# One-level products split by halves of a block's nodes, turns as 64 by 32 products, and two work banks, in a two-layer graph kernel

## What is computed

```python
def _L0_gnn_ref(x, L_scaled, weight, bias):       # K = 4
    Tx_prev2, Tx_prev1 = x, L_scaled @ x
    out = Tx_prev2 @ weight[0] + Tx_prev1 @ weight[1]
    for k in range(2, K):
        Tx_curr = 2.0 * (L_scaled @ Tx_prev1) - Tx_prev2
        out = out + Tx_curr @ weight[k]
        Tx_prev2, Tx_prev1 = Tx_prev1, Tx_curr
    return out + bias
def _L1_gnn_ref(x, adj, kernel, bias):
    support = adj @ poincare_expmap(x, 1.0)
    return poincare_logmap(support, 1.0) @ kernel + bias
h = jnp.maximum(_layernorm(x, axis=-1), 0.0)
x = x + _L0_gnn_ref(h, adj, L0_gnn_weight, L0_gnn_bias)
h = jnp.maximum(_layernorm(x, axis=-1), 0.0)
x = x + _L1_gnn_ref(h, adj, L1_gnn_kernel, L1_gnn_bias)
```

## Time and profile before

| | |
|---|---|
| median of 3 runs | 1762.29 us (1762.16 to 1763.82) |
| profiled execution | 1763.04 us, of which the span is 1760.9 us |
| PE busy | 1712.7 us (97% of the span) |
| DVE busy | 1276.1 us (72%) |
| ACT, POOL busy | 251.1 us (14%), 166.8 us (9%) |
| loads of blocks | 626 of 1 MB, queue's share of the DMA engines 93.9% |
| mean granted TensorE clock | 0.996 |

### The profile page before, as it was taken

The page is one execution under the profiler, slowest core; times in us unless marked ns, Lnnn a source line. Parts: engine busy times, 40 slices in busy tenths (PEclk is TensorE's granted clock), DMA queues, the critical chain, the costliest instruction groups (busy, mean ns, idle before and its releaser), DMA issues.

```text
span 1760.9 us, 57416 instructions
## 1 busy us (share of the span) xinstructions
PE 1712.7 (97%) x26188; PEld 940.1 (53%) x26188; DVE 1276.1 (72%) x1948; ACT 251.1 (14%) x468; POOL 166.8 (9%) x229
## 2 busy tenths in 40 slices
PE   7979999999999999999999999999999999999997
PEld 4423456666666665566666654345555444454444
DVE  7102686776888687688888886588878877786856
ACT  1000111111211011121110002222110110010024
POOL 0001000000000011211011000111001100010003
PEclk9999999999999999999999999999999999999999
DMA  9999999999999987889999986799999999999995
GB/s 371 421 421 421 420 419 419 411 409 419 402 402 394 400 298 274 335 321 330 339 332 336 338 329 267 288 362 395 419 419 419 418 416 416 418 407 419 419 420 230
DMA packets 94976, 664.54 MB, mean 377 GB/s; under 512 B 11408, under 2 KB 13712, under 8 KB 14608
## 3 DMA queue, kind: packets, MB, share of 16 engines
q1 hardware_dynamic: 93744, 660.64, 93.9%
q10 hardware_dynamic: 992, 0.23, 0.1%
HBM read 658.74 MB, written 2.10 MB: 375 GB/s over the span
## 4 chain that ended last, share of the span: by engine, by line
PE 81%; DVE 8%; DMA 8%; issue 2%; SPq 1%; POOL 0%; DVEq 0%; ACT 0%
PE own_bank L768 23%; PE row_bank L768 15%; PE work_bank L823 14%; PE row_bank L701 10%; PE work_bank L768 9%; DMA ring<-adj_blocks 8%; PE turned L900 2%; DVE ring L1081 2%; PE row_bank L808 1%; DVE ring L1085 1%; PE work_bank L784 1%; PE own_bank L844 1%; PE work_bank L844 1%; PE work_bank L712 1%; DVE partial L1116 1%
## 5 line engine op out<-in xcount | busy, mean ns | idle before, releaser
L1081 DVE TENSOR_TENSOR ring<-ring 128x1024 f32<-128x1024 f32 x318 | 392.9, 1236 | 106.7 <-PE own_bank L768 42.3
L768 PE MATMUL own_bank<-ring 128*32 128x256 f32 x4960 | 427.9, 379 | 0.3
L768 PE MATMUL own_bank<-ring,nodes 128*32 128x256 f32 x3720 | 380.8, 379 | 1.3 <-DVE ring L1081 1.3
L823 PE MATMUL work_bank<-ring,nodes 128*32 128x512 f32 (+1 forms) x2744 | 324.9, 593 | 6.8 <-DVE nodes L1274 5.1
L768 PE MATMUL row_bank<-ring 128*32 128x256 f32 x3488 | 300.4, 379 | 0.1
L768 PEld LDWEIGHTS own_bank<-ring 128*32 128x32 f32 x4960 | 246.3, 110 | 91.2 <-DVE ring L1085 2.2
L701 PE MATMUL row_bank<-ring,nodes 128*32 128x512 f32 (+1 forms) x1712 | 264.1, 597 | 19.1 <-DMA ring<-adj_blocks 16.1
L768 PE MATMUL row_bank<-ring,nodes 128*32 128x256 f32 x2616 | 266.3, 379 | 2.6 <-POOL ring L647 1.7
L768 PEld LDWEIGHTS own_bank<-ring,nodes 128*32 128x32 f32 x3720 | 201.9, 110 | 101.5 <-issue 43.9
L1085 DVE TENSOR_TENSOR ring<-ring 128x512 f32<-128x512 f32 x318 | 227.3, 715 | 10.9
L1087 DVE TENSOR_TENSOR ring<-ring 128x512 f32<-128x512 f32 x318 | 226.6, 713 | 10.9
(11 more groups left out here) (159 smaller groups left out, 1175.6 us busy)
## 6 DMA issues: line engine op xcount, KB each, us to landing
ring<-adj_blocks SPq DMA_DIRECT2D x626, 1024.0 KB, 11.3
out<-resid SPq DMA_DIRECT2D x16, 128.0 KB, 2.1
resid<-x SPq DMA_DIRECT2D x7, 256.0 KB, 12.0
resid<-x SPq DMA_DIRECT2D x2, 128.0 KB, 3.9
w_raw<-cheb_weight ACTq DMA_DIRECT2D x2, 64.0 KB, 8.4
bias<-cheb_bias ACTq DMA_DIRECT2D x1, 32.0 KB, 3.5
bias<-hyp_bias ACTq DMA_DIRECT2D x1, 32.0 KB, 3.9
w_raw<-hyp_kernel ACTq DMA_DIRECT2D x2, 16.0 KB, 9.3
```

The lines of the kernel that those rows point to most:

```text
L768: done = nc.tensor.matmul(bank[lane:lane + H, columns], left(a, h, level), right[b][:, h, :], start=first and k < 2, stop=k == 6, tile_pos ...
L823: done = nc.tensor.matmul(bank[lane:lane + size, :], nodes[:, c * C + k, A if level == 3 else B, part:part + size], data[:, k, :], start=k ...
L1081: nc.vector.tensor_tensor(first_two(n, block), block[:, :, N2].rearrange("p (k h) n -> p k h n", k=2), block[:, 0:2, :].rearrange("p h (k ...
```

## The change

1. One-level visits put nodes 0 to 255 of the row into partitions 0 to 63 and nodes 256 to 511 into 64 to 127, each with all four chunks summed: 16 products of 256 columns where there were 8 of 512, into half a bank. Sums of one level are so 128 by 256 in place of 128 by 512 or 64 by 512; where `partial` keeps a level by halves of the partitions (levels 1 to 3) an add becomes two of 64 by 256 (`to_levels`, `to_halves`).
2. ScalarE's copies at SUM and OWN are gone, with their semaphore; VectorE does the whole of `acc`, which is half as large.
3. A turn, and H_TERM, is 16 products of 64 by 32: both halves of the partitions at once, into the two banks of a pair, over two chunks each in place of four chunks one after the other.
4. There are two work banks; the third is the second bank of `turned`, which is used by AGAIN visits alone, and only with no turn within two visits. A bank with an OWN or column-13 visit is held until its JOIN. Level 4 turns have three pairs of banks where there were five banks.
5. Panels begin at rows 2, 4, 8 and 12. Level 1 has 38 JOINs where there were 24, with 323 fast visits in place of 318 and 7 plain BOTH visits in place of 12. The slots for sums are given up after row 0.
6. In the third sweep the OWN visits of rows 5 to 7 stand at the row's end as those of rows 8 and later do, EXPAND's features count as known one visit later, and the JOIN of level 3 adds in the kept sum.

The core of the diff:

```diff
-PANEL, FAST_BELOW, FAST_FROM, LATE_FROM = 4, 12, 5, 8
+FAST_BELOW, FAST_FROM, LATE_FROM = 12, 5, 8
+PANELS = (2, 4, 8, 12)
...
         def expand():
-            follow(1, ("EXPAND", row), known_now)
+            follow(1, ("EXPAND", row), lambda: follow(1, None, known_now))
...
-            visits_to_turn = 5
+            visits_to_turn = 5 if row < NB - 1 else 4
...
-            for v in [("OWN", k, c) for c in own_columns(k) if k < LATE_FROM] +
-            [("BOTH", k, c) for c in both_columns(k)] + [("OWN", k, c) for c in reversed(own_columns(k)) if k >= LATE_FROM]]
+            for v in [("OWN", k, c) for c in own_columns(k) if k < FAST_FROM] +
+            [("BOTH", k, c) for c in both_columns(k)] + [("OWN", k, c) for c in reversed(own_columns(k)) if k >= FAST_FROM]]
...
+            between = kind == "AGAIN" and i < first_out and not any(n - 2 < t < n + 2 for t in turn_at)
+            free = [k for k in range(2) if pair_ended and held_until[k] < i] + [2] * between
+            bank = min(free or [2], key=lambda k: bank_user[k][1] if bank_user[k] else -1)
...
+            def by_node_halves(bank, level, first, last):
+                for k in range(C):
+                    for half in range(2):
+                        for part in range(0, F, size):
+                            lane = half * F + part
+                            done = nc.tensor.matmul(bank[lane:lane + size, N1], nodes[:, c * C + k, level, part:part + size],
+                                                    data[:, k, half * 2 * P:(half + 1) * 2 * P], start=first and k == 0,
+                                                    stop=last and k == C - 1, tile_position=(0, lane))
+                return done
...
+            def to_nodes(pair, source, weight):
+                width = weight.shape[-1]
+                for k in range(2):
+                    for lane in range(0, P, TURN_SIZE):
+                        for half, rows in enumerate((ODD, EVEN)):
+                            at, to = k * P + lane, (1 - half) * (BLOCK - 2 * width) + k * width
+                            done = nc.tensor.matmul(pair[lane:lane + TURN_SIZE, half, to:to + width],
+                                                    source[rows, at:at + TURN_SIZE], weight[rows, :], start=k == 0, stop=k == 1,
+                                                    tile_position=(half * F, lane), skip_group_check=True)
+                return done
...
+            def to_halves(to, by_levels, level, by_halves, op=ALU.add):
+                for half, nodes_half in ((ODD, N1), (EVEN, N2)):
+                    done = nc.vector.tensor_tensor(to[half, :], by_levels[level, nodes_half], by_halves[half, N1], op)
+                return done
...
-                        nc.vector.tensor_tensor(acc[ODD, buf % 2, :], partial[ODD, r, :], bank[ODD, :], ALU.add)\
-                            .then_inc(s_acc, 1)
+                        to_halves(acc[:, buf % 2, :], partial[:, r, :], ODD, bank).then_inc(s_acc, 1)
...
+                        if level == 3 and r < NB - 1:
+                            step(last_sum)
...
+                            last_sum = nc.vector.tensor_tensor(joined[ODD, :], joined[ODD, :], partial[ODD, r, :], ALU.add)
```

More of the change, by code:

```diff
@@ L337, in chebyshev_hyperbolic_kernel @@
     last_visit_of = [0] * len(first_step_of)
-    own_pair_begun, own_pair_ended, last_own = False, False, None
+    pair_ended, last_own, turned_by = False, None, None
+    turn_at = [sum(t[0] in VISITS for t in steps[:i]) for i, s in enumerate(steps) if s[0] == "TURN"]
+    first_out = next(i for i, s in enumerate(steps) if s[0] == "TURN" and s[2] == 4)
     for i, s in enumerate(steps):
@@ L364, in chebyshev_hyperbolic_kernel @@
                 ("SPILL", i, spill_no[i])
+            if kind == "OWN" or i in plain:
+                held_until[bank] = steps.index(("JOIN", s[1], phase_of[i] + 1, 0))
             work_bank[i] = bank
         last_own = s[1] if kind == "OWN" else last_own if kind not in VISITS else None
-        if i in group_of and group_of[i] == 0 and not own_pair_begun:
-            own_pair_begun = True
-            pair_before = max(u[2] for u in bank_user[1:])
         if kind == "JOIN" and s[2] == 1 and group_no[s[1:]] == groups_first - 2:
-            own_pair_ended = True
-            bank_user[1:] = [("PAIR", i, groups_first - 2)] * 2
+            pair_ended = True
+            bank_user[:2] = [("PAIR", i, groups_first - 2)] * 2
         if kind == "TURN":
@@ L375, in chebyshev_hyperbolic_kernel @@
             turn_no[s[1:]] = turns
[L377 removed]
+            turn_before[i] = bank_user[2][2] if bank_user[2] and bank_user[2][0] == "SPILL" else 0
+            bank_user[2] = ("TURN", i, turns)
+    room_from = max(n for i, n in visit_no.items() if i < steps.index(("SUM", PANELS[0] - 2, 1)))
     sums_from = {2: room_from, 3: max(visit_no[i] for i in fast if phase_of[i] == 0),
@@ L464, in chebyshev_hyperbolic_kernel @@
     by_vector = list(batches[-1])
-    new_halves, last_spill_of, begun = {}, {}, set()
+    begin_sums, last_spill_of, begun = set(), {}, {(r, 2) for r in range(1, NB)} | {(r, 4) for r in range(LOW + 1, NB)}
     for i, s in enumerate(steps):
         if s[0] == "AGAIN":
[L471 to L476, removed]
+            if (s[1], s[3]) not in begun:
+                begin_sums.add(i)
+            begun.add((s[1], s[3]))
+            last_spill_of[s[1], s[3]] = spill_no[i]
     ctx = ExitStack()
@@ L840, in _ @@
                     pe.wait_ge(s_landed[slot], landed)
-                    for k in range(C):
-                        for part in range(2):
-                            lane = k % 2 * F + part * H
-                            done = nc.tensor.matmul(bank[lane:lane + H, :],
-                                                    nodes[:, c * C + k, A, part * H:(part + 1) * H], data[:, k, :],
-                                                    start=first and k < 2, stop=last and k >= 2, tile_position=(0, lane))
+                    done = by_node_halves(bank, A, first, last)
                     done.then_inc(s_visit, 1)
```

333 lines of the change are left out of this document (139 added, 194 removed).

## The result

The change makes the kernel slower: median 1769.91 us against 1762.32, ratio 1.0043 (95% interval 1.0033 to 1.0053). I had forecast 1753.3, with 1745 to 1767 as the range. The profiled execution has a span of 1768.2 us, 7.3 more than before.

What follows compares the result with a forecast made beforehand. PE was taken to bound the kernel until about 1232 us, saturated loads after, with loads also binding the changed first sweep. Terms -4.8 + 0.8 - 3.6 + 1.2 - 3 + 2 - 1.6 = -9.0 us gave 1753.3, range 1745 to 1767.

Steps and rivals of the forecast that it cites:

- Part 1: First sweep: panels from row 2 let fast visits begin earlier; row 7's add at 414 us, -4.8 us (-7.7 to -1).
- load 158 lands at 409.5: First sweep, new order: the load row 7's SUM needs lands at 409.5 us, so PE, arriving at 411, runs into the loads.
- PE waits 6.4 us in all: First sweep, old order: PE's waits for loads up to row 7's SUM total 6.4 us, with arrival at 419.6.
- The walk: First sweep: stepping through visits with chain prices and load landing times; row 7's SUM at 419.6 old order, 411 new.
- The line: First sweep's loads: load n lands at 16.1 + 2.49 n us, from three waits at loads 34, 45 and 66.
- Part 2: One-level visits: twice the records, 1.726 us against 1.717, some 85 visits where PE decides, +0.8 us.
- 54 ns each: Fast visits: 56 records of 256 columns in 3.02 us, the rate used to price one-level visits with 32 records.
- Part 3: Turns: 0.72 us instead of 0.87, -3.6 us (-10 to +6.7); level 3 turns 0.62, +1.2 us (-1.6 to +2).
- rival A: Turns: row halves run one after the other, a turn takes 1.15 us; +16.5 us on the forecast, 1770 us, chance 0.10.
- Part 4: Third sweep up to 1232 us: shorter level 4 adds and moved OWN visits relieve DVE, -3 us (0 to -6).
- Part 5: Two work banks: AGAIN visits wait for a bank between sweeps, around 1104 us and at row ends, +2 us (0 to +8).
- Part 6: Tail, 1711 to 1744 us: shorter turns leave the loads deciding, last add and turn shorter, -1.6 us (-3 to +4.7).

## Why the prediction was wrong, step by step

**Part 1, the first sweep: -4.8 forecast at row 7's add; +4.2 measured, and +1.0 with the panels alone.** The step that failed is "load 158 lands at 409.5", together with "PE waits 6.4 us in all". Load 158 (counted from 0) is the last that row 7 needs, in all three kernels. It landed at 414.85 in the kernel before, at 415.76 with the panels alone and at 417.65 in the changed kernel. From load 66 to load 158 a load takes 2.55 us in each of the three, 412 GB/s, and not 2.49. The loads of that stretch land 10 to 16 us after their issue, so several were always under way, and 412 is not PE's pace. Why the loads ran at 412 isn't shown; the sign was in the earlier trace rows, where slices 8 and 9 (308 to 396 us) read 411 and 409, while the prediction read "419 to 421 GB/s in slices 2 to 8". In the kernel before, the add stood 4.1 us behind load 158's landing, and with the panels it stands 4.2 behind. So row 7 hung on its loads already, and a shorter sum of PE gained nothing there.

The walk hid this. I had begun PE's sum at 31.1 us with the first visit, but six visits lie ahead of it, 10 us that were counted twice. In the run of before with a quarter of the loads left out, PE goes from that visit (31.43) to row 7's add (402.55) in 371 us, where the sum has 382. With the 10 us off, the waits for loads are 16.7 us and not 6.4, which fits the 16.4 us between that add and the one at 418.90. The walk still gave 419.6, because the two errors, a line of landings too early and a sum of PE too long, nearly cancelled at that mark: luck, which I took for agreement. The line had been tested only up to load 66. I also left out that fast blocks are wanted two visits ahead. Of the 6 us between 414 and 419.93, the landing is 3.3 (415.76 against 412.5, the line with the 3.0 that I had added), and the rest is the longer way from that landing to the add. Why load 158 landed 1.9 us later still in the changed kernel, and the add stood 5.4 us behind it, is open.

**Part 2, one-level visits: +0.8 forecast; here the forecast broke.** "The records double" was costed by PE's streaming alone, and a steady 54 ns a record seemed proof that issue keeps up. The trace shows that fast visits run at 112 instructions in 3.02 us, 256 in 6.9, and the tail of before at 32 + 64 in 2.59 us, again 256 in 6.9. Both are just slower than the 6.2 to 6.5 us between the waits. The changed tail wants 128 in 2.46 us, 256 in 4.9. Where the pace stays above that for longer than the store of fetched instructions lasts, PE waits: 5.3 us in the last 45, 2.9 at 1090 to 1113 and 0.9 in the first 62. The steady part is 1.73 in place of 1.717, at most 4 us over all 340 visits, where I had counted 85 of them. So the step that failed is the one from "54 ns each" to "+0.8 us": the price of an instruction was taken from its streaming, and its supply was put at nothing. Splitting visits alone cost 12 us.

The Trainium skill states this supply (Runtime: NRT & Kernel Launch, Instruction fetch mechanics): instructions come in blocks of 16 KiB, 256 each, by the sequencer's own DMA queue, and it says that this is hidden, since issue is slower than the fill. The packets of 16 KB and the distance of 256 instructions agree with it. That it is hidden does not hold here: PE issues up to 64 instructions in 0.60 us, and the waits are up to 1.76 us.

**Part 3, turns: the price was right.** Forecast 0.72, measured 0.60 + 0.13 = 0.73; level 3 forecast 0.62, measured 0.38 + 0.14 = 0.52. The two parts of that price were not: I had 0.435 for the products and 0.28 for two switches, and it is 0.60 and 0.13. The halves of the rows run beside each other. The second sweep, with the 16 turns of level 2, is 1.9 us shorter, where I had 2.4 for them (from row 15's add of level 1 to the last add of the second sweep, at 1079.32 before, it took 390.4 and takes 388.5). So rival A, which alone gave a slower kernel, is false. That its 1770 us is the measured time is chance: the kernel is slower for a reason that I didn't have. The product shape of 32 columns is what made the gain unreachable; at 64 columns it is there.

**Part 4, the third sweep: the way was right, the size isn't shown.** Forecast -3, and DVE is busy 6.3 us less at 1166 to 1232. From the last add of the second sweep to the mark it took 152.3 us (1079.32 to 1231.59), takes 154.0 in the changed kernel with its 2.9 us of waits for instructions, and 150.2 with turns of 64 by 64 (1077.50 to 1227.65). That -2.1 holds the turns of level 3 and the visits too; no run takes part 4 by itself.

**Part 5, two banks: right in size.** Forecast +2 (0 to +8). It is 1.54 us in each of two places and 0.5 in each of two others. With the turns of 64 by 64, the wait at row 10 ends just as the JOIN has read the bank that OWN held:

```profile
1371.99 0.85 DVE L1026 TENSOR_TENSOR acc<-joined,work_bank 64x256 f32<-64x256 f32 x2
1372.95 1.93 PE L690 MATMUL work_bank<-ring,nodes 128*32 128x256 f32 x32 [1.54 <-issue]
```

It is named issue too, and the place alone does not tell the two kinds apart, since a wait for instructions can fall before a whole piece too (1741.97 in the run with split visits). The length and the packets do: this wait is 1.54 us in every run of the changed kernel, with all loads or half of them, and ends anywhere from 0.4 to 4.4 us behind a packet's start. That the bank is what it waits for is read from the time of the JOIN's add; no run with a third bank shows it.

**Part 6, the tail: -1.6 forecast, +5.7 measured** (from row 15's add to the end of the last turn: 58.2 us before, 63.8 after). It is -1.4 with turns of 64 by 64 (56.7 us). So it is the instructions that broke this step.

The marks together, as differences to the kernel before in us of the span:

| mark (in the kernel before) | forecast | changed kernel | with turns of 64 by 64 |
|---|---|---|---|
| row 7's add, level 1 (418.90) | -4.8 | +4.2 | +3.4 |
| row 15's add, level 1 (688.93) | | +1.0 | 0.0 |
| last add of the second sweep (1079.32) | | -0.9 | -1.8 |
| mark of the third sweep (1231.59) | -7.4 | +0.9 | -3.9 |
| row 15's last add of level 3 (1691.62) | | +1.1 | -3.9 |
| end of the span (1760.9) | -9.0 | +7.3 | -5.1 |

Of the 16.6 us between the forecast and the measured median, 11 come back with half the instructions in each turn and nothing else changed. Between the profiled executions it is 12.4: 7.4 behind row 15's last add, 4.8 before 1232. The 3.5 us that are still missing at 1231.59 are about what part 1 had promised and the panels don't give.

## What to carry to other kernels

Count instructions per microsecond as a resource of its own: program bytes arrive by the same DMA engines as the data, and here PE was fed about 256 instructions in 6.3 us while the loads were full, and 256 in 4.9 us without a wait once they had ended. When a product is cut smaller at equal streaming time, compare that pace before and after, above all in the stretch that ends the kernel. Choose the widest tile that leaves the queues equally long: 64 by 64 in place of 64 by 32 cost nothing and turned 7.6 us of loss into 3.7 us of gain.

A walk that reproduces old marks can do so with two errors that cancel. Compare its parts with the trace as well: the landing of the loads near the mark, and the sum of the waits. Before the order is changed, take one resource away in one run and see the other's sum by itself.

## What the runs showed of the hardware

Products of 64 rows in the two halves of the array run beside each other: 32 records of 128 columns in 0.60 us against 0.87. A switch of product shape costs 0.13 to 0.15 us: the visit behind a turn takes 1.86 in place of 1.73, and in the run with 64 columns for all one-level visits 1.73 and 3.02 become 1.88 and 3.16.

PE's instructions come in packets of 16 KB by a DMA queue of their own. With full loads these started 6.1 to 6.6 us apart in the tail, with none 3.7 to 4.0. Where PE asked for more than that, it waited 0.2 to 1.8 us, each time until 2.3 to 2.6 us behind a packet's start. These waits came to 9.1 us with all loads, 6.0 with a quarter left out and 2.5 with half left out.
